# A fp32 residual stack on one core: activation blocks read back into 14 tiles, the first width block's order, the T sums and the LoRA B gather

## The reference, cut to what matters

```python
x = x + einsum('bct,bcd->bdt', x, W0[cond])                      # layer 0, 64x64 per batch
gate = x @ Wg.T + lora(x, A_gate, B_gate)                        # layer 1: H 1024 -> F 2752, rank 16
up   = x @ Wu.T + lora(x, A_up, B_up)
x = x + ((silu(gate) * up) @ Wd.T + lora(act, A_down, B_down))
x = x + s4d_convolution(x) * mask                                # layer 2, length 1024
x = x + einsum('bct,bcd->bdt', x, W3[subj]) + bias[subj]         # layer 3
```

## Time and profile before

| | us |
|---|---|
| median of 3 runs | 1801.99 |
| lowest, highest | 1799.14, 1804.69 |
| the profiled execution's own time | 1799.51 |
| its span, first to last instruction | 1798.0 |
| TensorE busy (matmul) | 1699.1 |
| VectorE, ScalarE, GpSimd busy | 1073.3, 645.3, 171.1 |
| mean granted TensorE clock, share of full | 0.982 |

### The profile page before, as it was taken

How to read it: one execution, slowest core, us unless ns; L and a number is a source line. 1 busy time by engine, 2 the same in 40 slices (tenths; PEclk the granted TensorE clock), 3 DMA queues, 4 the chain that set the end, 5 groups by cost and what they waited for, 6 DMA issues and landing times.

```text
span 1798.0 us, 27548 instructions
## 1 busy us (share of the span) xinstructions
PE 1699.1 (95%) x8832; PEld 1455.2 (81%) x8832; DVE 1073.3 (60%) x1565; ACT 645.3 (36%) x988; POOL 171.1 (10%) x286
## 2 busy tenths in 40 slices
PE   5789999999996999998799999999989999999998
PEld 5668888888875888888588888888877888879997
DVE  4756666666655753634866666666643442338887
ACT  4333333333333433124433333333333242226665
POOL 4431000000002000000000000000025100003230
PEclk9799999999998999999899999999999999999999
DMA  8774333333336375474333333333245564467654
GB/s 281 262 257 143 106 115 99 94 93 96 96 109 206 105 238 172 126 260 158 106 94 93 93 99 102 110 108 94 70 153 181 170 201 122 143 206 240 243 188 188
DMA packets 127210, 270.71 MB, mean 151 GB/s; under 512 B 24822, under 2 KB 35990, under 8 KB 126902
## 3 DMA queue, kind: packets, MB, share of 16 engines
q1 hardware_dynamic: 117126, 249.87, 43.8%
q0 software_dynamic: 9712, 20.10, 3.4%
q10 hardware_dynamic: 320, 0.07, 0.0%
HBM read 226.17 MB, written 63.21 MB: 161 GB/s over the span
## 4 chain that ended last, share of the span: by engine, by line
PE 82%; DVE 6%; DMA 5%; SPq 2%; ACT 2%; issue 2%; DVEq 0%; POOL 0%; ACTq 0%; POOLq 0%
PE ps L1171 42%; PE ps L1254 23%; PE ps L1346 5%; PE ps L1181 4%; PE ps L1343 3%; DMA ast<-act_dram 2%; DVE wlo L1576 2%; ACT whi L859 1%; PE ps L1374 1%; DMA raw<-bgu_of_batches 1%; PE ps L1104 1%; PE ps L1268 1%; PE ps L1271 1%; DMA raw<-in_agu 1%; PE ps L1359 1%
## 5 line engine op out<-in xcount | busy, mean ns | idle before, releaser
L859 ACT ACTIVATE whq<-rq 128x512 fp32r<-128x512 f32 x294 | 184.2, 630 | 510.3 <-PE ps L1171 418.4
L1645 DVE TENSOR_TENSOR wlq<-rq,whq 128x512 fp32r<-128x512 f32 x294 | 201.6, 687 | 226.0 <-ACT whq L859 226.0
L1254 PE MATMUL ps<-act_hi,whi 128*128 128x512 f32 x672 | 266.6, 397 | 23.4 <-DVE wlo L1576 23.4
L1576 DVE TENSOR_TENSOR wlo<-raw,whi 128x1536 fp32r<-128x1536 f32 (+2 forms) x84 | 131.5, 1574 | 257.9 <-ACT whi L859 257.7
L1254 PE MATMUL ps<-act_lo,whi 128*128 128x512 f32 x672 | 264.4, 393 | 0.0
L1254 PE MATMUL ps<-act_hi,wlo 128*128 128x512 f32 x672 | 264.0, 393 | 0.0
L859 ACT ACTIVATE whi<-raw 128x1536 fp32r<-128x1536 f32 (+3 forms) x96 | 115.9, 1219 | 396.2 <-PE ps L1254 290.2
L1171 PE MATMUL ps<-b_hi,whq 128*128 128x512 f32 x504 | 201.2, 399 | 29.3 <-DVE u L1655 15.0
L1171 PE MATMUL ps<-b_lo,whq 128*128 128x512 f32 x504 | 199.9, 397 | 0.0
L1171 PE MATMUL ps<-b_hi,wlq 128*128 128x512 f32 x504 | 198.5, 394 | 0.0
L1171 PE MATMUL ps<-t_hi,whq 128*128 128x512 f32 x504 | 196.6, 390 | 0.0
(11 more groups left out here) (255 smaller groups left out, 2887.0 us busy)
## 6 DMA issues: line engine op xcount, KB each, us to landing
raw<-in_wd SPq DMA_DIRECT2D x176, 256.0 KB, 3.2
rtoep<-k_dram SPq DMA_DIRECT2D x64, 512.0 KB, 4.6
rq<-in_wq SPq DMA_DIRECT2D x42, 768.0 KB, 7.1
lraw<-bgu_of_batches SPq DMA_DIRECT2D x84, 256.0 KB, 7.0
act_dram<-c SPq DMA_DIRECT2D x84, 256.0 KB, 2.0
ast<-act_dram SPq DMA_DIRECT2D x84, 256.0 KB, 4.8
rq<-in_wq SPq DMA_DIRECT2D x42, 256.0 KB, 4.3
bgu_of_batches<-in_bgu POOLq DMA_DIRECT2D x30, 352.0 KB, 6.1
```

Source lines behind the costliest of these rows:

```text
L859: return act.activation(dst, src, ACT.Copy)
L1254: ins = pe.matmul(ps[:, g * 4 + h, :], wt[i][:, kk * 4 + h, :], a[k][:, :], start=k == 0 and n_ == 0, stop=False)
L1576: ins = tt(w_low, r, f32(w_high), ALU.subtract)
L1645: tt(wlq[o][:, :, :], rq[par][:, o, :, :], f32(whq[o][:, :, :]), ALU.subtract).then_inc(w_lo, 1)
```

## The change

- **Act blocks.** For even chunks, `load_act` fills 14 tiles `act_raw` in the place of both `rq` buffers, once the last block's operands are split (`w_lo`). Odd chunks keep the three tiles `ast`. The order of loads around the last block changes.
- **First width block.** VectorE's part of block 0 is written out: `sum_u2`, `sum_u3`, `sum_c22a` and block 1's splits are placed before and around the rest columns; `rt` is two tiles, and the wait for `rest_out` moves to VectorE, to `sum_c21`.
- **T sums.** T3 and T4 get tiles of their own (`t3s`, `t4s`, hi and lo places swapped), each sum and each hi copy waits for its own store; for s = 1, T1 and T3 are summed inside `down(1)`. RM multiplies its second half first, so that T1 may be written early.
- **LoRA.** LA2 and LA3 get raw buffers of their own. Of B, 10 of 44 column blocks are gathered first (80 of 352 KB a batch), the other 34 after POOL's constants; SP issues none of them, and waits for the second part after the third width block.

```diff
-            def gather_b_0():
...
+                back = 4 if GS_OF.get(n % NU) in ("RM", "RL") else 2
+                if n >= back:
+                    sp.wait_ge(lo_done[n % 2], (n - back) // 2 + 1)
...
             def load_act(c, k):
+                if c % 2 == 0:
+                    i, done = k % 14, F0(c // 2) + (FULL if k == FULL - 1 else FULL - 1)
+                    if k >= 14:
+                        sp.wait_ge(act_lo_done, c * FB + k - 13)
+                    dst, landed = act_raw[:, i, :], act_in[i]
...
             def start(s):          # sync
+                    load_lora_a(0, 2)
                     load_x(7)
+                    load_rest(0)
                     load_lora_a(0, 3)
                     sp.wait_ge(l0_hi, 8)
+                    store_x0(0, B11)
+                    store_x0(0, B21)
                     sp.wait_ge(l0_hi, 16)
+                    store_x0(0, B12)
                     load_operands(0, 0, 0)
                     load_rest_lora(0)
+                    store_x0(0, B22)
...
             def gate_up_last(s):   # sync
+                sp.wait_ge(w_lo, fg * 7 + 7)
+                for k in range(ACT_FIRST):
                     load_act(c, k)
                 sp.wait_ge(prod, fg * 7 + 3)
                 load_down_unit(c, 0)
+                for k in range(ACT_FIRST, 14):
                     load_act(c, k)
                 sp.wait_ge(prod, fg * 7 + 6)
                 load_down_unit(c, 1)
+                store_act(c, FULL - 1, fg)
+                for k in range(14, 18):
                     load_act(c, k)
                 store_act(c + 1, FULL - 1, fg)
...
+                    if s == 0 and f == 2:
+                        sp.wait_ge(bgu_in[1], 2 * CB * 16)
...
+            for grp in range(4):   # gpsimd, after the constants
+                with pool.Fori(0, HB) as b:
+                    gather_b_gate_up(0, grp, b, lora_key(b + grp * HB), bgu_in[1], slice(B_FIRST, GU + 1))
...
             def start(s):          # scalar
+                act.wait_ge(t_sum, 4 * s + 2)
+                act.wait_ge(x0_out[B12], 16 * (s + 1))
+                hi_t(T3, t3s[:, :, :])
+                act.wait_ge(t_sum, 4 * s + 3)
+                act.wait_ge(x0_out[B22], 16 * (s + 1))
+                hi_t(T2, x32[B11][:, :, :])
                 hi(n + 5, "RL")
...
             def start(s):          # vector, s = 0 from here, then both
                     lo(n + 3, "LA3")
+                    sum_t1(0)
+                    lo(n + 4, "RM")
+                    sum_t3(0)
                     lora_t(0, 2)
+                    sum_t2(0)
                     lora_t(0, 3)
+                    lo_t(0, 1, T3, t3s[:, :, :])
+                    sums_of_a(0, 0)
                     lo(n + 5, "RL")
...
+                sum_t4(s)
+                lo_t(s, 2, T2, x32[B11][:, :, :])
+                lo_operand(fg, 0, 0)
+                lo_operand(fg, 0, 1)
+                lo_t(s, 3, T1, t1[:, :, :])
...
+                sum_u2(fg)
+                lo_t(s, 4, T4, t4s[:, :, :])
+                lo_lora(fg)
+                lo_operand(fg, 0, 5)
+                sum_u3(fg)
+                sum_c22a(fg)
+                lo_operand(fg, 0, 6)
+                sums_of_a(fg + 1, 1)
+                lo_operand(fg + 1, 1, 0)
+                lo_operand(fg + 1, 1, 1)
+                sum_c22(fg)
+                lo_operand(fg + 1, 1, 2)
                 for part in range(2):
+                    tt(rt[part][0:REST, :], rt[part][0:REST, :], ps[REST:P, 4 + part, :],
+                       ALU.mult).then_inc(rest_act, 1)
+                lo_operand(fg + 1, 1, 3)
+                sum_c21(s, fg)     # waits for rest_out, 32 * (s + 1)
```

More of the change, by code:

```diff
@@ L170, in build @@
                                   for i, n in enumerate("u2 c22 g11 c21 c12".split()))
-        rt = tile("rt", [P, TOK], F32, T0 + 8192)
+        rt = [tile(f"rt{i}", [P, TOK], F32, T0 + 8192 - i * 2048) for i in range(2)]
         xr = tile("xr", [P, 5, TOK], F32, T0)
@@ L239, in build @@
         raw_in = [sem(f"raw_in{i}") for i in range(2)]
+        la_in = [sem(f"la_in{i}") for i in range(2)]
+        act_in = [sem(f"act_in{i}") for i in range(14)]
+        b12_read = sem("b12_read")
         hi_done = [sem(f"hi_done{i}") for i in range(2)]
@@ L439, in load_lora_a @@
                 n = gs(s, f"LA{j}")
-                unit_free(n)
+                if j < 2:
+                    unit_free(n)
+                elif s == 1 and j == 3:
+                    m15 = du(1, DO.index("M15"))
+                    sp.wait_ge(unit_done[m15 % 2], m15 // 2 + 1)
                 w = 2 * KB * RANK
+                buffer = raw[:, j, :, :] if j < 2 else la_raw[j - 2][:, :, :]
+                landed = (raw_in if j < 2 else la_in)[j % 2]
                 for b in range(HB):
@@ L600, in gate_up_last @@
                 c, fg = 2 * s, LAST_F[s]
-                for k in range(7):
+                sp.wait_ge(w_lo, fg * 7 + 7)
+                for k in range(ACT_FIRST):
                     load_act(c, k)
@@ L625, in down @@
                         load_lora_a(1, p + 2 - len(DO))
-                    if c % 2 == 0 and p < 4:
-                        for k in act_prep_after(c, p + 1):
+                    if c % 2 == 0 and p < 2:
+                        for k in range(18 + 2 * p, 20 + 2 * p):
                             load_act(c, k)
@@ L650, in down @@
                         load_x_pieces()
+                    if c == 1 and p == 18:
+                        load_lora_a(1, 2)
                     if c == 1 and p >= 16:
@@ L676, in _ @@
                 start(s)
-                with sp.Fori(0, 9) as j:
+                for f in range(4):
+                    gate_up(s, f, F0(s) + f, f % 2, True)
+                    if s == 0 and f == 2:
+                        sp.wait_ge(bgu_in[1], 2 * CB * 16)
+                with sp.Fori(2, 9) as j:
                     for par in range(2):
@@ L891, in hi @@
                 i, m = n % 2, n // 2
-                act.wait_ge(raw_in[i], raw_count(n))
+                if name in ("LA2", "LA3"):
+                    act.wait_ge(la_in[i], 64 * (n // NU + 1))
+                else:
+                    act.wait_ge(raw_in[i], raw_count(n))
                 if m > 0:
@@ L1043, in _ @@
                 start(s)
-                with act.Fori(0, FULL // 2) as j:
+                gate_up(s, 0, F0(s), 0, True)
+                gate_up(s, 0, F0(s) + 1, 1)
+                with act.Fori(1, FULL // 2) as j:
                     for par in range(2):
@@ L1141, in start @@
                     pe.wait_ge(res_done, 14)
-                for ch in range(2):
+                for ch in (1, 0):
                     for k in range(KB):
@@ L1850, in down @@
                         lo_x(1, range(4 * (p - 16), 4 * (p - 16) + 4))
+                    if c == 1 and p == 18:
+                        sum_t1(1)
+                        sum_t3(1)
                     r = residual_after(c, p)
```

231 lines of the change are left out of this document (112 added, 119 removed).

## The result

The changed kernel takes 1744.8 us (median of 4, 1742.7 to 1746.1), beside 1802.4 of the kernel before in the same comparison: ratio 0.9681, 95% interval 0.9662 to 0.9699. It is faster, inside the range of 1716 to 1750, and 15 us slower than the 1730 forecast. The profiled execution took 1746.1, its span is 1744.6, against 1798.0: 53.4 us less.

A forecast was written before the change was run, and what follows sets the result against it. TensorE bounds the kernel; winnable are its idle time and lower-clock matmuls, in two starts and two passages into the down stage. Gains 22.5 + 18 + 19 + 11 = 70.5 us give 1729.0, stated as 1730, range 1716 to 1750.

The forecast's parts named there:

- LA2 to RM: In start(0), LA2 starts at 36.3, 5.7 us earlier, no longer waiting for a buffer; LA3 about 40, RM about 43.8.
- RL at 58.4, product 0 at 63.7: In start(0), VectorE's path of 14.6 us sets RL; product 0 comes at 63.7 instead of 79.13, 15.4 earlier.
- rule on turns between queues: DMA engines alternate queues packet by packet; second gathers halve the B22 store's rate, landing at 56, 2 us worse.
- Block 0: First width block: the 8.16 us `sum_u2` wait and 2.0 of cold clock go; a 2.2 us cold start may stay.
- I take 1.5: After block 0, the moved `rest_out` wait puts `sum_u2(1)` at 97 to 101, needed at 98: 0 to 3 us stall.
- start(1): Start of s = 1: product 0 at 867.7 instead of 875.87; gain 18 us in all, bounds 12 and 21.5.
- Stretch 3: First passage from last width block into the down stage: act loads go out together; gain 19 us, bounds 13 to 21.
- Stretch 4: Second passage from last width block into the down stage: gain 11 us, bounds 8 to 12.5.
- At nothing: Parts priced at zero: added wait at `sum_c21` in the loop, 16 added gathers (26 us on POOL), written-out blocks.
- rival of 1815: The gathers' second part stops SP after the third block; about 1815 us at 13 us a gather; chance 0.02.
- the starts give half: Late transfers hold VectorE's and ScalarE's new order: 8 us in first start, 6 in second, 3 elsewhere: 1747; chance 0.17.
- It does not do what it says: `sum_u2` still waits, ScalarE's copy of product 0 standing behind other copies; 8 to 16 us stay: 1742; chance 0.05.

The follow-up runs named there:

- e2: Changed kernel with B22's store issued before SP's wait for the 16 small gathers and RL's load, not behind them: 1742.1 us.
- e5: Changed kernel with the split of the gathers undone, all 44 columns in the first 16 gathers and no second ones: 1756.0 us.
- e1: Changed kernel with block 1's LoRA load issued ahead of the two rest stores in each start: 1733.4 us.
- e7: Changed kernel with the act part undone, three act tiles and SP's old load order: 1772.6 us.
- e10: Changed kernel with 14 act tiles and SP's old load order, but M1's weights ahead of the last full block's store: 1751.8 us.

## Why the prediction was right, and where not

The direction, the range and the four places were right. The forecast itself, "1722 to 1738 alone" with 0.63, was missed: 1744.8 lies inside the range because the range took in a rival with a chance of 0.17. Of the signs of being wrong that the prediction names, two came: RL after 62 (62.91), and a wait of over 3 us for weights after M0 (the 3.12 us in chunk 2, for a late split). The forecast was 17.2 us too good (70.5 against 53.3 in the four stretches of the profiled execution), by these steps:

- *LA2 to RM.* As put: LA2 right behind the last layer 0 unit, LA3 and RM at 40.8 and 44.2 (about 40 and 43.8).
- *RL at 58.4, product 0 at 63.7.* VectorE's sum of 14.6 held, but the step "landing at 54 gives RL's copy at 57, in time" failed. The gathers' last landing was 49.5, not 47, and B22's store landed at 58.7, inside the bounds of 52 and 62. Product 0 came 4.3 late, in a stretch that scatters: it starts between 65.4 and 70.9 in the nine traces with this code. e2's edit gets 2 to 3 of it back. The rule on turns between queues, priced at 2 us, is not settled: beside the second gathers the store took 7.3 us, but in the same code also 5.7 to 8.5, and in e5, which has no second gathers but those for down instead, 11.2. No run has the store without GpSimd's gathers beside it.
- *Block 0.* Both `sum_u2` waits went. The 2.2 us for a cold start were not needed: product 0 to block 1 took 21.1 us, so 2.1 came back. The 1.5 us taken off for unknown landings (22.5 for 24) were needed.
- *"I take 1.5" for what is late next.* This term failed, in both starts: 8.5 us (5.80 and 2.7 of lower clock) and 6.1 (3.33 and 2.7, where "about 1" stood). The prediction counted what is queued behind the wait on VectorE, and it did name "block 2's operands and block 1's LoRA behind these stores" on SP, but gave that no price. e1 shows that most of the loss was there (11.5 us), and that the wait it did price is nearly free alone. This is 7.0 + 5.1 of the 17.2.
- *start(1) apart from that.* Product 0 at 868.2 on the old axis, forecast 867.7.
- *Stretch 3.* 18.0 for 19: the waits for weights of down are 3.9 us in 4, not 2.0. The sum was right, its reason only in part: "each load waits for a split and then takes its whole latency" describes the tiles, and e7 to e10 give them 6.5 to 9.4 us. The larger piece, 11.4 to 14.3, is M1's place ahead of a store that waits, which the prediction only had as a time ("M1's after product 5 at 529.6").
- *Stretch 4.* 8.2 for 11. The collision with GpSimd costs 3.12 us of wait and some 2.8 of matmuls 0.43 apart instead of 0.23, less the 1.06 of before: 4.9. Without it the stretch would have been 2 us better than forecast.
- *At nothing.* SP never waited for the second gathers, whose last is issued at 76.07 and wanted at about 150. The rival of 1815 had no part in it.
- *Of the rivals*, "the starts give half" was the nearest (1747), and its mechanism is what held: RL's neighbours and a load behind the rest stores land late. Its price for the starts, 8 + 6, was close to what was missing, 7.6 + 5.8; that its total also fits is partly luck, since its 3 us for the rest have another cause, mostly the addition. "It does not do what it says" is untrue by its place (`sum_u2` of block 0 is on time), but the same wait came back one block later.

Open is what the raw buffers of LA2 and LA3, the new places of T3 and T4 and the early sums of T1 and T3 for s = 1 are worth alone: none of the runs undid them.

## What to carry to other kernels

When a wait is moved, price every entry behind it in the queue of the engine that issues the loads, not only the work behind it on the engine that computes: here two DMA issues, 1.2 us together, cost 11.5 us, and one pair of lines swapped (weights ahead of a store that waits for a late product) is worth 11 to 14. A reordering and a second buffer that cure the same stall are tried one at a time; here the buffer sufficed, and the new order, by where it put the multiplications, lost 11 us. When a stage is made faster, look for what runs beside it by its own clock, as GpSimd's addition here: it will fall on another, less patient step.

## What the runs showed of the hardware that was not expected

- GpSimd issues 16 gathers of 80 KB in 27.2 us (17.97 to 45.19) and 16 of 352 KB in 24.7 (18.34 to 43.01): the pace does not follow the bytes. Within the small ones it varies from 1.6 to 2.4 us; why was not found.
- A 1.76 us `tensor_tensor` of VectorE took 4.0 to 5.2 beside one of GpSimd and ended 1.5 to 1.6 us after it, in all 14 traces; the profile reports TensorE's wait for it as "issue", with no releaser, in 11 of them.
